# Gate weights broadcast in pieces, a projection in another order, and an attention core whose second pass begins at another tile

## The chip, the cores and the metric

One core of one Trainium2 chip runs a two-layer model (eight residual stages) on 4 x 1024 tokens of width 128, in float32 with some bf16 operands. The metric is the device time of one execution in microseconds. The three runs of the kernel before took 3448.38, 3451.47 and 3469.87 us.

## The reference, cut to what matters

Each stage reads the normalised x and adds its result to x. The change touches three of the stages: the first attention, the mixture-of-experts FFN (used twice) and the latent attention's projection.

```
x = x + L0_attn_a(layernorm(x))   # 64 batch-heads, causal, scores + a table by distance
x = x + L0_ffn(layernorm(x))      # stage f0
x = x + L0_attn_b(layernorm(x))
x = x + L0_ffn(layernorm(x))      # stage f1
x = x + L1_attn_a(layernorm(x))   # latent attention, rotary part
...
def L0_ffn(x):                    # 8 experts, top 2, and a shared expert
    logits = x @ gate_w.T
    idx = top_2(logits + lb_bias)
    w = sigmoid(logits[idx]); w = w / (sum(w) + 1e-6)
    hidden = square(relu(x @ w1[e]))            # for every expert e
    return sum_e(we[e] * (hidden @ w2[e])) + square(relu(x @ cfc)) @ cproj
def L1_attn_a(x):
    c_q, c_kv = x @ W_DQ, x @ W_DKV
    Q = concat(c_q @ W_UQ, rope(c_q @ W_QR)); K = concat(c_kv @ W_UK, rope(x @ W_KR)); V = c_kv @ W_UV
```

## The kernel before

Every stage is a block in which the five engines run lists written out by hand, tied by counting semaphores (a wait holds up everything behind it on its engine). Between blocks there is a barrier. Tokens go in 8 groups of 512; x stays in SBUF.

**First attention core** (`attention_two_pass`, L1028; tiles named l0aa). The 64 batch-heads go in 16 quads of 4. A first pass finds for each query the lowest score: per quad 18 tiles, each a set of matmuls into a bank of 128x1024 (`first_pass`, L1183) and one reduction on DVE (`first_lows`, L1346, L1350). Eight small reductions, a transpose and three parts in bf16 (`second_lows`, `parts`, `remainder`, `remainder_low` with L1377) turn the result into rows that a DMA puts under the queries. The second pass has 36 steps a quad (`second_pass`, L1221): scores into one of three banks, Exp on ACT (L1322) for three heads of four, then a multiplication by the table on POOL (L1179: one instruction for heads 0 and 1, one for head 2); for the fourth head DVE adds the table first (L1344). `weigh` multiplies by v. The lists of PE and DVE place one tile of the next quad's first pass in every second step, 20 steps ahead (AHEAD); so before step 0 all 18 tiles of quad 0 and 10 tiles of quad 1 are done.

**FFN of layer 0** (`l0_ffn`, L340; f0 and f1). Per group: normalisation (`ln_first`, `ln_second`), a transpose, logits, a gate of 18 small DVE steps (`gate_first`, `gate_second`, `gate_weights`), and `weights_T`, `to_weT`: the gate weights, transposed, go to DRAM (L388) and come back broadcast to all partitions in one DMA of 2 MB (L392, wB). For each of 9 units n: `up` on PE, `relu` and `square` on ACT, `weigh` by wB on DVE (L458), `down` on PE three units later. Groups 0 and 1 are gated before the loop; group g + 2 is gated within group g. In f0, SP first issues the loads of the next stage's weights and of the layer-1 FFN's (`ahead`: L998, L143), then serves the gate weights.

**Latent projection** (`l1a_project`, L2703; l1ap). Per group: PE makes the latents (pL), rotary parts (pR, pS), q, k, v and the transposes of the next group's x; DVE normalises the next group, combines the rotary parts (t1, t2, L2801 and L2802) and with ACT splits q, k and r into three bf16 parts, which SP sends to DRAM (L1010; in four groups it also loads heads, L2881).

Of the kernel before, what the change touches and what calls it, by code (L numbers as in the profile page):

```python
# [17 lines left out]
ACT = mybir.ActivationFunctionType  # L18
# [83 lines left out]
def ln_group_vector(nc, dve, src, out, S, steps, rough_ready, rough_want, ve_ready):  # L102

    for k in range(GROUP_BLOCKS):
        ins = nc.vector.bn_stats(S["st"][:, k, :], src(k))  # L105
    steps.done(ins)
    ln_variance(nc, S, steps, ve_ready)
    ln_newton(nc, dve, S, steps, rough_ready, rough_want)
    return ln_apply(nc, src, out, S)

# [229 lines left out]
def l0_ffn(nc, D, x, C, tag, we_dram, ahead=None):  # L340
# [6 lines left out]
    with ExitStack() as ctx:  # L347
# [27 lines left out]
        we_out, we_in = [sem("we_out0"), sem("we_out1")], [sem("we_in0"), sem("we_in1")]  # L375
# [5 lines left out]
        @block.sync  # L381
        def _(sp):
            if ahead is not None:
                ahead(sp)
            for g in range(GROUPS):
                par = g % 2
                sp.wait_ge(weT_ready, g + 1)
                sp.dma_start(we_dram[par], weT[:, par, :]).then_inc(we_out[par], 16)  # L388
                sp.wait_ge(we_out[par], 16 * (g // 2 + 1))
                if g >= 2:  # L390
                    sp.wait_ge(wb_used, (g - 1) * E)
                sp.dma_start(wB[:, par], we_dram[par:par + 1].broadcast_to([P, E, GROUP])).then_inc(we_in[par], 16)  # L392
# [8 lines left out]
        def _(dve):  # L401
# [49 lines left out]
            def weigh(g, e):  # L451
                n = g * HT + e
                dve.wait_ge(s_ready, n + 1)
                if e == 0:
                    dve.wait_ge(we_in[g % 2], 16 * (g // 2 + 1))
                if n >= RING:
                    dve.wait_ge(hT_used, n - RING + 1)
                nc.vector.tensor_tensor(hT[:, n % RING, :], rT[:, n % RING, :], wB[:, g % 2, e, :], ALU.mult).then_inc(wb_used, 1)  # L458
# [6 lines left out]
            for gn in (0, 1):  # L465
                lns, gs = Steps(dve, ln_step, LN_STEPS, gn), Steps(dve, g_step, G_STEPS, gn)
                ln_first(lns, gn)
                ln_second(lns, gn)
                gate_first(gs, gn)
                gate_second(gs)  # L470
                gate_weights(gs, gn)
# [26 lines left out]
        def _(act):  # L498
# [38 lines left out]
            to_weT(1)  # L537
            for n in range(3, N):
                relu(n)
                g, f = n // HT, n % HT  # L540
                if f == 1 and 1 <= g and g + 1 < GROUPS:
                    to_weT(g + 1)
                square(n)
                if g + 2 < GROUPS:
                    if f == 4:
                        to_xt(g + 2)
                    if f == 6:
                        gate_sigmoid(g + 2)

        @block.tensor  # L550
        def _(pe):
# [50 lines left out]
            weights_T(1)  # L602
            for n in range(3, N):
                g, f = n // HT, n % HT
                up(n)
                down(n - LAG)
                if g >= 1 and f == 1 and g + 1 < GROUPS:
                    weights_T(g + 1)
                if g + 2 < GROUPS:
                    if f == 3:  # L610
                        transposes(g + 2)
                    if f == 5:
                        logits(g + 2)
# [414 lines left out]
def attention_two_pass(nc, C, D, tag, qs, ks, qd, kd, qm, km, table, rows, v_all, cx, den, mask):  # L1028
# [38 lines left out]
    ADDED = 3  # L1067
    with ExitStack() as ctx:
# [113 lines left out]
        def _(pe):  # L1182
# [75 lines left out]
            for t in range(AHEAD // 2):  # L1258
                first_pass(1, t)
                if t == 1:  # L1260
                    turn_lows(0)
            for n in range(RING - 1):
                second_pass(n)
            for n in range(N):
                if n % 2 == 0:
                    quad, t = (n + AHEAD) // STEPS + 1, (n + AHEAD) % STEPS // 2
                    if quad < QUADS:
                        first_pass(quad, t)
                if n + RING - 1 < N:
                    second_pass(n + RING - 1)  # L1270
                if n % STEPS == STEPS - AHEAD + 3 and n // STEPS + 1 < QUADS:
                    turn_lows(n // STEPS + 1)
                if n % QUAD == 3 and n >= 2 * QUAD - 1:
                    weigh(n // QUAD - 1)
# [62 lines left out]
        def _(dve):  # L1337
# [44 lines left out]
            for t in range(AHEAD // 2):  # L1382
                first_lows(1, t)
                if t == 1:
                    remainder(0)
                    remainder_low(0)
            for n in range(N):
                after, more = n % STEPS - (STEPS - AHEAD), n // STEPS + 1 < QUADS
                if after == 0 and more:
                    second_lows(n // STEPS + 1)  # L1390
                if n % 2 == 0:
                    quad, t = (n + AHEAD) // STEPS + 1, (n + AHEAD) % STEPS // 2
                    if quad < QUADS:
                        first_lows(quad, t)
                if after == 5 and more:
                    remainder(n // STEPS + 1)
                if after == 8 and more:
                    remainder_low(n // STEPS + 1)
                if n % QUAD == ADDED:
                    add_table(n)  # L1400
# [1302 lines left out]
def l1a_project(nc, D, x, C, tag, v_all, dram, ahead):  # L2703
# [3 lines left out]
    with ExitStack() as ctx:  # L2707
# [17 lines left out]
        xt = sb("xt", [P, GROUP])  # L2725
# [57 lines left out]
        def _(dve):  # L2783
            for par in (0, 1):
                dve.sem_inc(sent[par], 16 * SENDS)
            def layernorm(gn, par):
                steps = Steps(dve, ln_step, LN_STEPS, gn)
                dve.wait_ge(xT_done, gn + 1)
                ln_group_vector(nc, dve, lambda k: x[:, bass.ds((gn + 1) * GROUP_BLOCKS + k, 1), :], xn[:, par], S, steps,
                                ln_rough, gn + 1, ln_ve).then_inc(xn_ready, 1)  # L2790
                steps.close()

            layernorm(0, 0)
            dve.wait_ge(w_in, 16 * NW)
            with dve.Fori(0, BATCH) as b:
                for par in (0, 1):
                    g = b * 2 + par
                    t = slice(par * GROUP, (par + 1) * GROUP)
                    layernorm(g + 1, 1 - par)
                    dve.wait_ge(done["r"], g + 1)  # L2800
                    nc.vector.tensor_tensor(t1[:], pR[0:R, :], cos[:, t], ALU.mult)  # L2801
                    nc.vector.tensor_tensor(t2[:], pS[0:R, :], sin[:, t], ALU.mult).then_inc(rope, 1)  # L2802
                    dve.wait_ge(rope, g + 2)
# [14 lines left out]
        def _(act):  # L2818
            def to_xt(gn):
                act.wait_ge(xT_done, gn + 3)  # L2820
                nc.scalar.activation(xt[:], pT[:], ACT.Copy).then_inc(xt_ready, 1)

            to_xt(0)
            with act.Fori(0, BATCH) as b:
                for par in (0, 1):
# [5 lines left out]
                    for n in "qk":  # L2831
                        act.wait_ge(done[n], g + 1)
                        nc.scalar.activation(part[n][:, par, 0, :], src[n][:], ACT.Copy).then_inc(hi[n], 1)
                    act.wait_ge(r_ready, g + 1)
# [4 lines left out]
                    to_xt(g + 1)  # L2839

        @block.tensor
        def _(pe):
# [11 lines left out]
            with pe.Fori(0, BATCH) as b:  # L2854
                for par in (0, 1):
                    g = b * 2 + par
                    pe.wait_ge(xt_ready, g + 1)
                    nc.tensor.matmul(pL[0:L, :], wl[:], xt[:], start=True, stop=True).then_inc(lat_done, 1)
# [9 lines left out]
                    nc.tensor.matmul(pK[:], wuk[:], lat[:], start=True, stop=True).then_inc(done["k"], 1)  # L2868
                    pe.wait_ge(v_ready, g + 1)
# [3 lines left out]
                    transposes(g + 1, 1 - par)  # L2873
# [298 lines left out]
def build(nc, D, out):  # L3172
    with ExitStack() as ctx:
# [39 lines left out]
        with ExitStack() as stages:  # L3213
# [3 lines left out]
            def ahead(sp):  # L3217
                load_l0_attn_b(sp, D, C, W)
                load_l1_ffn(sp, D, C)

            l0_ffn(nc, D, x, C, "f0", we, ahead=ahead)
            l0_attn_b(nc, D, x, C, W, "l0b")
        l0_ffn(nc, D, x, C, "f1", we)
# [113 lines left out]
```

## Time and profile before

| | us |
|---|---|
| median of 3 runs | 3451.47 (3448.38 to 3469.87) |
| profiled execution: time, span | 3457.46, 3455.7 |
| first attention core, second pass | 236 to 757 |
| f0, f1 | 900 to 1077, 1396 to 1560 |
| latent projection | 1560 to 1676 |
| mean TensorE clock of the span | 0.93 of full |

All times are from the start of the span of one profiled execution. PE is TensorE's matmuls, PEld its weight loads, DVE VectorE, ACT ScalarE, POOL GpSimd, SP SyncE. In a timeline a row stands for one instruction or for a run of like ones (x8), with the idle time of the engine just before it in brackets and what ended that. [...]

### The profile page before, as it was taken

The page shows a single profiled execution, that of the slowest core. Times are in us where ns is not written, and L with a number is a line of the kernel's source. Part 1 is how long each engine was busy: PE and PEld are TensorE (multiplying, and loading weights), DVE is VectorE, ACT ScalarE, POOL GpSimd, SP SyncE. Part 2 cuts the span into 40 slices and gives each one's busy share as a digit, 9 for nine tenths or more (in the row PEclk, how much of TensorE's full clock was granted, in tenths as well). Part 3 has the DMA queues.
Part 4 walks back from the last instruction along what each step waited for, and adds up shares of the span by engine and source line. Part 5 has one row for each costly group of instructions (what it writes and reads, how often), then busy time and mean ns, then how long its engine had stood idle before and what let it go on. Part 6 is the DMA issues. An engine that isn't in the chain of part 4 may idle for free. (4 is left out here: it accounts for less than half of the span.)

```text
span 3455.7 us, 67058 instructions
## 1 busy us (share of the span) xinstructions
PE 3053.0 (88%) x25109; PEld 1677.9 (49%) x25109; DVE 2373.2 (69%) x5084; ACT 1862.5 (54%) x3317; POOL 945.4 (27%) x655
## 2 busy tenths in 40 slices
PE   6778999958599999896799969998999999999899
PEld 3234444423276555573222237764455555555676
DVE  6578888848574554666799942235999999998321
ACT  5336666642264332463599924443666666666444
POOL 1029999971001322000000000001222223232100
PEclk8779999989798999897799969999999999999999
DMA  5212333210330000224322210017434344332000
GB/s 169 71 63 94 106 118 109 91 54 24 104 123 25 1 1 1 99 99 157 106 68 67 62 44 1 1 35 219 112 88 99 98 105 106 97 100 68 12 10 13
DMA packets 215138, 260.69 MB, mean 75 GB/s; under 512 B 45211, under 2 KB 165604, under 8 KB 212497
## 3 DMA queue, kind: packets, MB, share of 16 engines
q1 hardware_dynamic: 214849, 256.83, 25.0%
q8 instruction: 183, 3.00, 0.4%
q14 instruction: 106, 0.86, 0.1%
HBM read 200.72 MB, written 56.55 MB: 74 GB/s over the span
## 5 line engine op out<-in xcount | busy, mean ns | idle before, releaser
L1179 POOL TENSOR_TENSOR l0aa_e<-l0aa_e,l0aa_et 128x1024 f32<-128x1024 f32 (+1 forms) x288 | 512.0, 1816 | 44.6 <-ACT l0aa_e L1322 44.5
L2597 ACT ACTIVATE l1ba_sg<-l1ba_sg,l1ba_mn 128x128 f32<-128x128 f32 (+7 forms) x512 | 394.4, 774 | 185.3 <-DVE l1ba_mn L2649 184.2
L2649 DVE CUSTOM_DVE_ANT_0 l1ba_sg<-l1ba_pS,l1ba_tab 128x128 f32<-128x128 f32 (+7 forms) x512 | 368.0, 743 | 40.9 <-PE l1ba_pS L2538 28.5
L1350 DVE TENSOR_REDUCE l0aa_low<-l0aa_pP 128x8 f32<-128x1024 f32 x288 | 343.2, 1220 | 65.8 <-PE l0aa_pP L1203 61.8
L2659 DVE STREAM_TRANSPOSE l1ba_pT<-l1ba_sg 128x1024 f32<-128x1024 f32 (+3 forms) x344 | 367.1, 1067 | 18.5 <-ACT l1ba_sg L2597 13.5
L319 PEld LDWEIGHTS f_pY<-l_w,f_hT 128*128 128x128 f32 x2048 | 268.8, 192 | 122.9 <-issue 119.5
L2559 PE MATMUL l1ba_pO<-l1ba_pT,l1ba_v 32*64 32x256 f32 x9216 | 320.0, 389 | 7.8 <-ACT l1ba_y L2612 7.8
L3027 ACT ACTIVATE l1aa_e<-l1aa_e 128x1536 f32<-128x1536 f32 x192 | 284.4, 1483 | 33.3 <-DVE l1aa_e L3070 21.0
L282 ACT ACTIVATE f_hT<-f_pH,l_b 128x512 f32<-128x512 f32 x256 | 173.9, 687 | 237.4 <-PE f_pH L311 237.2
L2482 POOL TENSOR_TENSOR l1ba_co<-l1ba_co,l1ba_rb 128x1024 f32<-128x1024 f32 x64 | 151.5, 2367 | 544.3 <-ACT l1ba_co L2605 512.5
L1322 ACT ACTIVATE l0aa_e<-l0aa_pS 128x512 f32<-128x512 f32 x432 | 243.0, 593 | 87.0 <-PE l0aa_pS L1236 48.4
L319 PE MATMUL f_pY<-l_w,f_hT 128*128 128x128 f32 x2048 | 269.9, 275 | 0.7 <-ACT f_hT L282 0.7
L311 PE MATMUL f_pH<-f_xt,l_w 128*128 128x512 f32 x512 | 268.1, 608 | 0.0
L2559 PEld LDWEIGHTS l1ba_pO<-l1ba_pT,l1ba_v 32*64 32x64 f32 x9216 | 176.5, 132 | 177.4 <-issue 144.4
L3070 DVE SCALAR_TENSOR_TENSOR l1aa_e<-l1aa_pS,l1a_ceiling 128x1536 f32<-128x1536 f32 x128 | 214.8, 1749 | 5.6 <-PE l1aa_pS L2987 5.6
L1233 PE MATMUL l0aa_pS<-l0a_qs,l0a_ks 128*128 128x512 bf16 (+3 forms) x768 | 191.3, 332 | 30.6 <-DVE l0aa_e L1344 16.8
L1196 PE MATMUL l0aa_pP<-l0a_ks,l0a_qs 96*128 96x512 bf16 (+3 forms) x768 | 186.5, 347 | 28.0 <-DVE l0aa_rest L1372 13.4
L2987 PE MATMUL l1aa_pS<-l1a_qs,l1a_ks 72*128 72x512 bf16 (+3 forms) x768 | 165.5, 341 | 38.1 <-DVE l1aa_e L3068 13.6
L2538 PE MATMUL l1ba_pS<-l1b_k,l1ba_qs 64*128 64x448 f32 (+2 forms) x768 | 178.5, 545 | 17.8 <-DVE l1ba_mn L2649 17.8
L590 PEld LDWEIGHTS f_pY<-l_w,f_hT 128*128 128x128 f32 x1152 | 152.4, 194 | 79.0 <-issue 64.7
L1250 PE MATMUL l0aa_pO<-l0aa_e,l0aa_vh 128*32 128x512 f32 (+3 forms) x1536 | 155.1, 499 | 10.6 <-POOL l0aa_e L1179 10.6
L590 PE MATMUL f_pY<-l_w,f_hT 128*128 128x128 f32 x1152 | 153.1, 278 | 10.8 <-DVE f_hT L458 10.8
(407 smaller groups left out, 5103.2 us busy)
## 6 DMA issues: line engine op xcount, KB each, us to landing
f_wB<-l0f_weights SPq DMA_DIRECT2D x16, 2048.0 KB, 7.2
l1ba_rb<-l1b_rdd SPq DMA_DIRECT2D x64, 512.0 KB
l0aa_et<-l0a_table SPq DMA_DIRECT2D x16, 1536.0 KB
l1b_qd<-l1bp_part SPq DMA_DIRECT2D x64, 256.0 KB, 2.4
l1ba_qs<-l1b_qd SPq DMA_DIRECT2D x48, 256.0 KB
l0aa_et<-l0a_table SPq DMA_DIRECT2D x16, 512.0 KB
l1ba_tab<-l1b_table SPq DMA_DIRECT2D x32, 256.0 KB
l1ba_qs<-l1b_qd SPq DMA_DIRECT2D x64, 128.0 KB
```

The lines of the kernel that those rows point to most:

```text
L311: nc.tensor.matmul(pH[n % RING][:], w1[:, n % HT, :], xt[:, n // HT % 2, :], start=True, stop=True).then_inc(h_done, 1)
L319: ins = nc.tensor.matmul(pY[g % 2][:, k * P:(k + 1) * P], hT[:, n % RING, k * P:(k + 1) * P], w2[:, f, :], start=(f == 0 and k == 0), stop ...
L590: ins = nc.tensor.matmul(pY[g % 2][:, k * P:(k + 1) * P], hT[:, n % RING, k * P:(k + 1) * P], w2[:, f, :], start=(f == 0 and k == 0), stop ...
L1179: nc.gpsimd.tensor_tensor(es, es, t, ALU.mult).then_inc(multiplied, heads)
L1322: nc.scalar.activation(e[:, n % E_SLOTS, :], pS[n % RING][:], ACT.Exp, scale=-1.0).then_inc(e_done, 1)
L1350: nc.vector.tensor_reduce(low1[:, t, :], pP[TURN[quad, t]][:].rearrange("p (u t) -> p u t", t=P), AX.X, ALU.min).then_inc(p1_low, 1)
L2559: ins = nc.tensor.matmul(pO[a][part * HALF:(part + 1) * HALF, 0:HG * Q], v4[a * Q:(a + 1) * Q, group_of(r)[0] % 2, (SEQ - width(r)) // Q + ...
L2597: nc.scalar.activation(row, row, ACT.Exp, bias=mn[:, r % 2, i + k:i + k + 1], scale=-1.0, accum_out=den[:, r % 2, i + k:i + k + 1]).then_i ...
L2649: nc.vector.tensor_tensor_reduce(row, scores, bias, 1.0, 3e38, ALU.add, ALU.min, mn[:, r % 2, h:h + 1]).then_inc(m_done, 1)
L2659: nc.vector.transpose(pT[tile][:, c + i * width(r):c + (i + heads) * width(r)], sg[:, n % RING, 0:heads * width(r)]).then_inc(t_done, 1)
L3027: nc.scalar.activation(es, es, ACT.Exp, scale=1 / ROOT).then_inc(e_done, 1)
L3070: ins = nc.vector.scalar_tensor_tensor(es, pS[s % 2][:], -CLIP, ceiling[:, unit - 1, :], ALU.max, ALU.min)
```

## The change

Three edits. In the attention core, 6 tiles of quad 1's first pass (before: 10) precede step 0, and steps 0 to 7 hold one tile each; from step 8 on the order is as before. In `l0_ffn`, wB comes in four DMAs of two experts with a semaphore each; DVE computes group 1's statistics before group 0's gate; `weights_T(1)` moves from before unit 3 to unit 4, and in group 0 the transposes and logits of group 2 move two units later; the `ahead` loads are issued after the last gate weights, those of the layer-1 FFN now in f1. In `l1a_project`, DVE's normalisation is cut in two around t1 and t2, the transposes precede v, xt has two buffers, and the copy to it comes before the r part on ACT.

```diff
@@ l0_ffn
-        we_out, we_in = [sem("we_out0"), sem("we_out1")], [sem("we_in0"), sem("we_in1")]
+        we_out = [sem("we_out0"), sem("we_out1")]
+        we_in = [[sem(f"we_in{par}_experts{e}") for e in range(0, E, 2)] for par in (0, 1)]
...
-            if ahead is not None:
-                ahead(sp)
             for g in range(GROUPS):
...
-                sp.dma_start(wB[:, par], we_dram[par:par + 1].broadcast_to([P, E, GROUP])).then_inc(we_in[par], 16)
+                for e in range(0, E, 2):
+                    sp.dma_start(wB[:, par, e:e + 2], we_dram[par:par + 1, e:e + 2].broadcast_to([P, 2, GROUP])).then_inc(we_in[par][e // 2], 16)
+            ahead(sp)
...
-                if e == 0:
-                    dve.wait_ge(we_in[g % 2], 16 * (g // 2 + 1))
+                if e % 2 == 0:
+                    dve.wait_ge(we_in[g % 2][e // 2], 16 * (g // 2 + 1))
...
-            for gn in (0, 1):
-                lns, gs = Steps(dve, ln_step, LN_STEPS, gn), Steps(dve, g_step, G_STEPS, gn)
-                ln_first(lns, gn)
-                ln_second(lns, gn)
-                gate_first(gs, gn)
-                gate_second(gs)
-                gate_weights(gs, gn)
+            lns, gs = ([Steps(dve, step, n, gn) for gn in (0, 1)] for step, n in ((ln_step, LN_STEPS), (g_step, G_STEPS)))
+            ln_first(lns[0], 0)
+            ln_second(lns[0], 0)
+            ln_first(lns[1], 1)
+            gate_first(gs[0], 0)
+            gate_second(gs[0])
+            gate_weights(gs[0], 0)
+            ln_second(lns[1], 1)
+            gate_first(gs[1], 1)
+            gate_second(gs[1])
+            gate_weights(gs[1], 1)
@@ l0_ffn, scalar
             gate_sigmoid(1)
-            to_weT(1)
             for n in range(3, N):
                 relu(n)
                 g, f = n // HT, n % HT
-                if f == 1 and 1 <= g and g + 1 < GROUPS:
+                if f == (1 if g else 4) and g + 1 < GROUPS:
                     to_weT(g + 1)
                 square(n)
                 if g + 2 < GROUPS:
-                    if f == 4:
+                    if f == (4 if g else 6):
                         to_xt(g + 2)
-                    if f == 6:
+                    if f == (6 if g else 7):
                         gate_sigmoid(g + 2)
@@ l0_ffn, tensor
             logits(1)
-            weights_T(1)
             for n in range(3, N):
                 g, f = n // HT, n % HT
                 up(n)
+                if n == 4:
+                    weights_T(1)
                 down(n - LAG)
...
-                    if f == 3:
+                    if f == (3 if g else 5):
                         transposes(g + 2)
-                    if f == 5:
+                    if f == (5 if g else 7):
                         logits(g + 2)
@@ attention_two_pass
+    EARLY = 6
+    def tile_at(n):
+        if n < AHEAD - 2 * EARLY:
+            return 1, EARLY + n
+        if n % 2 == 0 and (n + AHEAD) // STEPS + 1 < QUADS:
+            return (n + AHEAD) // STEPS + 1, (n + AHEAD) % STEPS // 2
+        return None
... (tensor; vector has the same with first_lows)
-            for t in range(AHEAD // 2):
+            for t in range(EARLY):
                 first_pass(1, t)
...
-                if n % 2 == 0:
-                    quad, t = (n + AHEAD) // STEPS + 1, (n + AHEAD) % STEPS // 2
-                    if quad < QUADS:
-                        first_pass(quad, t)
+                if tile_at(n):
+                    first_pass(*tile_at(n))
@@ l1a_project
-        xt = sb("xt", [P, GROUP])
+        xt = sb("xt", [P, 2, GROUP])
... (vector)
-                    layernorm(g + 1, 1 - par)
+                    steps = Steps(dve, ln_step, LN_STEPS, g + 1)
+                    ln_statistics(nc, rows(g + 1), S, steps, ln_ve)
                     dve.wait_ge(done["r"], g + 1)
                     nc.vector.tensor_tensor(t1[:], pR[0:R, :], cos[:, t], ALU.mult)
                     nc.vector.tensor_tensor(t2[:], pS[0:R, :], sin[:, t], ALU.mult).then_inc(rope, 1)
+                    normalise(g + 1, 1 - par, steps)
                     dve.wait_ge(rope, g + 2)
... (scalar: after the two "hi" copies of q and k)
+                    to_xt(g + 1, 1 - par)
                     act.wait_ge(r_ready, g + 1)
...
                         nc.scalar.activation(part[n][:, par, 1, :], f[n][:], ACT.Copy).then_inc(mid[n], 1)
-                    to_xt(g + 1)
... (tensor)
                     nc.tensor.matmul(pK[:], wuk[:], lat[:], start=True, stop=True).then_inc(done["k"], 1)
+                    transposes(g + 1, 1 - par)
                     pe.wait_ge(v_ready, g + 1)
...
-                    transposes(g + 1, 1 - par)
@@ build
-            def ahead(sp):
-                load_l0_attn_b(sp, D, C, W)
-                load_l1_ffn(sp, D, C)
-
-            l0_ffn(nc, D, x, C, "f0", we, ahead=ahead)
+            l0_ffn(nc, D, x, C, "f0", we, lambda sp: load_l0_attn_b(sp, D, C, W))
             l0_attn_b(nc, D, x, C, W, "l0b")
-        l0_ffn(nc, D, x, C, "f1", we)
+        l0_ffn(nc, D, x, C, "f1", we, lambda sp: load_l1_ffn(sp, D, C))
```

## Rows read from the trace of the kernel before

**Rows 1.** Window over the second pass: length, busy PE, PEld, DVE, ACT, POOL, then PEclk.
```profile
236.00:757.00 521.00, 465.81 (x3744) 210.00 (x3741) 430.99 (x554) 344.58 (x648) 512.00 (x288) 0.98 0.28 91
```

**Rows 2.** Timeline of POOL, first attention core: start, us, instruction [idle before <-releaser].
```profile
236.34 27.17 POOL L1179 TENSOR_TENSOR l0aa_e<-l0aa_e,l0aa_et 128x1024 f32<-128x1024 f32 x15 [35.98 <-ACT l0aa_e L1322]
266.99 1.26 POOL L1179 TENSOR_TENSOR l0aa_e<-l0aa_e,l0aa_et 128x512 f32<-128x512 f32 x1 [3.47 <-ACT l0aa_e L1322]
269.82 3.60 POOL L1179 TENSOR_TENSOR l0aa_e<-l0aa_e,l0aa_et 128x1024 f32<-128x1024 f32 x2 [1.58 <-ACT l0aa_e L1322]
...
295.17 421.85 POOL L1179 TENSOR_TENSOR l0aa_e<-l0aa_e,l0aa_et 128x1024 f32<-128x1024 f32 x237 [0.26 <-ACT l0aa_e L1322]
```

**Rows 3.** Timeline of DVE, four stretches of the same stage.
```profile
225.93 9.95 DVE L1350 TENSOR_REDUCE l0aa_low<-l0aa_pP 128x8 f32<-128x1024 f32 x8 [0.51 <-PE l0aa_pP L1203]
...
257.95 5.71 DVE L1377 TENSOR_TENSOR l0aa_mp<-l0aa_rest,l0aa_mp 32x128 bf16<-32x128 f32 x1
...
296.95 0.72 DVE L1377 TENSOR_TENSOR l0aa_mp<-l0aa_rest,l0aa_mp 32x128 bf16<-32x128 f32 x1
...
707.54 9.62 DVE L1377 TENSOR_TENSOR l0aa_mp<-l0aa_rest,l0aa_mp 32x128 bf16<-32x128 f32 x1
```

**Rows 4.** Timelines of PE and ACT, the same stage.
```profile
234.41 1.06 PE L1233 MATMUL l0aa_pS<-l0a_qs,l0a_ks 128*128 128x512 bf16 x2
235.26 0.78 PE L1196 MATMUL l0aa_pP<-l0a_ks,l0a_qs 96*128 96x512 bf16 x3
...
254.94 1.08 ACT L1322 ACTIVATE l0aa_e<-l0aa_pS 128x512 f32<-128x512 f32 x2 [0.75 <-PE l0aa_pS L1236]
```

**Rows 5.** Timeline of all engines, start of f0 (SPq: SP's DMA issues).
```profile
911.67 9.61 SPq L143 DMA_DIRECT2D l_w<-in_L_ffn_w  x2
...
914.39 0.87 DVE L407 BATCH_NORM_STATS2 f_ln_stats<-x 128x6 f32<-128x128 f32 x4
...
915.39 0.57 ACT L511 ACTIVATE f_weT<-f_pT 8x512 f32<-8x512 f32 x1
...
926.69 0.19 DVE L448 TENSOR_TENSOR f_we<-f_sg,f_mx 128x32 f32<-128x32 f32 x1
...
929.62 0.33 SPq L388 DMA_DIRECT2D l0f_weights<-f_weT  x1
...
932.55 0.33 SPq L392 DMA_DIRECT2D f_wB<-l0f_weights  x1
...
939.76 0.69 DVE L458 TENSOR_TENSOR f_hT<-f_rT,f_wB 128x512 f32<-128x512 f32 x1 [11.35 <-DMA f_wB<-l0f_weights]
```

**Rows 6.** The same, second FFN.
```profile
1420.79 0.19 DVE L448 TENSOR_TENSOR f_we<-f_sg,f_mx 128x32 f32<-128x32 f32 x1
...
1422.41 0.69 DVE L458 TENSOR_TENSOR f_hT<-f_rT,f_wB 128x512 f32<-128x512 f32 x1
...
1430.27 0.97 PEld L565 LDWEIGHTS f_pG<-l_gw,f_xt 128*128 128x128 f32 x8
...
1432.95 0.69 DVE L458 TENSOR_TENSOR f_hT<-f_rT,f_wB 128x512 f32<-128x512 f32 x1
...
1434.90 0.69 DVE L458 TENSOR_TENSOR f_hT<-f_rT,f_wB 128x512 f32<-128x512 f32 x1
```

**Rows 7.** Timelines of DVE, PE and SP, latent projection: groups 2 and 3 of 0 to 7.
```profile
1598.01 0.16 DVE L89 TENSOR_TENSOR l1ap_ln_newton<-l1ap_ln_rstd 128x4 f32<-128x4 f32 x1 [1.12 <-POOL l1ap_ln_rstd L2776]
...
1599.84 0.68 DVE L2801 TENSOR_TENSOR l1ap_t<-l1ap_pR,l1ap_cos 68x512 f32<-68x512 f32 x1
...
1605.42 2.02 PE L2858 MATMUL l1ap_pL<-l1ap_xt,l1ap_wl 128*100 128x512 f32 x2 [3.71 <-ACT l1ap_xt L2821]
...
1606.49 2.24 SPq L1010 DMA_DIRECT2D l1a_kc<-l1ap_partk  x3
```

**Rows 8.** Windows over those two groups, columns as in the windows above.
```profile
1594.90:1605.40 10.50, 6.04 (x22) 2.92 (x22) 9.13 (x29) 4.73 (x8) 1.01 (x1) 0.95 0.61 190
1605.40:1618.80 13.40, 10.18 (x23) 4.13 (x23) 9.52 (x30) 4.46 (x8) 1.01 (x1) 0.66 0.83 281
```

More of the change, by code:

```diff
@@ L109, in ln_group_vector, with ln_statistics @@
     return ln_apply(nc, src, out, S)
+def ln_statistics(nc, src, S, steps, ve_ready):
+    for k in range(GROUP_BLOCKS):
+        ins = nc.vector.bn_stats(S["st"][:, k, :], src(k))
+    steps.done(ins)
+    ln_variance(nc, S, steps, ve_ready)
 LN_STEPS = 6
@@ L337, in _, with l0_ffn @@
                 down(n)
-def l0_ffn(nc, D, x, C, tag, we_dram, ahead=None):
+def l0_ffn(nc, D, x, C, tag, we_dram, ahead):
     E = 8
@@ L1381, in _ @@
             second_lows(0)
-            for t in range(AHEAD // 2):
+            for t in range(EARLY):
                 first_lows(1, t)
@@ L1390, in _ @@
                     second_lows(n // STEPS + 1)
[L1391 to L1394, printed above, removed]
+                if tile_at(n):
+                    first_lows(*tile_at(n))
                 if after == 5 and more:
@@ L2785, in _, with rows, normalise @@
                 dve.sem_inc(sent[par], 16 * SENDS)
-            def layernorm(gn, par):
-                steps = Steps(dve, ln_step, LN_STEPS, gn)
+            def rows(gn):
+                return lambda k: x[:, bass.ds((gn + 1) * GROUP_BLOCKS + k, 1), :]
+            def normalise(gn, par, steps):
+                ln_newton(nc, dve, S, steps, ln_rough, gn + 1)
                 dve.wait_ge(xT_done, gn + 1)
-                ln_group_vector(nc, dve, lambda k: x[:, bass.ds((gn + 1) * GROUP_BLOCKS + k, 1), :], xn[:, par], S, steps,
-                                ln_rough, gn + 1, ln_ve).then_inc(xn_ready, 1)
+                ln_apply(nc, rows(gn), xn[:, par], S).then_inc(xn_ready, 1)
                 steps.close()
-            layernorm(0, 0)
+            steps = Steps(dve, ln_step, LN_STEPS, 0)
+            ln_statistics(nc, rows(0), S, steps, ln_ve)
+            normalise(0, 0, steps)
             dve.wait_ge(w_in, 16 * NW)
@@ L2818, in _, with to_xt @@
         def _(act):
-            def to_xt(gn):
+            def to_xt(gn, par):
                 act.wait_ge(xT_done, gn + 3)
-                nc.scalar.activation(xt[:], pT[:], ACT.Copy).then_inc(xt_ready, 1)
-            to_xt(0)
+                nc.scalar.activation(xt[:, par, :], pT[:], ACT.Copy).then_inc(xt_ready, 1)
+            to_xt(0, 0)
             with act.Fori(0, BATCH) as b:
@@ L2857, in _ @@
                     pe.wait_ge(xt_ready, g + 1)
-                    nc.tensor.matmul(pL[0:L, :], wl[:], xt[:], start=True, stop=True).then_inc(lat_done, 1)
+                    nc.tensor.matmul(pL[0:L, :], wl[:], xt[:, par, :], start=True, stop=True).then_inc(lat_done, 1)
                     pe.wait_ge(rope, g + 1)
```

## The prediction, made before the change was run

> **What bounds the kernel now.** No engine bounds the whole span, so I read the three touched stages one by one: first the windows for the busiest engine, then that engine's timeline for what ended its idle time, then the engine that released it.
>
> In the attention core the window [rows 1] has PE at 466 of 521 us, but POOL at 512.0, and the timeline of POOL [rows 2] shows it without a pause for 421.85 us. PE's 466 is pipelined matmuls, so POOL is the bound: the stage lasts as long as POOL's start (236.34), its 512.0 of work, and its few pauses. They all follow one instruction. L1377, a 32x128 operation on DVE, takes 0.72 us at 296.95 but 5.71 at 257.95 and 9.62 at 707.54 [rows 3]; both long ones end just as POOL's run ends (27.17 us after 236.34), and POOL then sits idle 3.47 + 1.58 us for want of Exp output [rows 2]. DVE was held until POOL had run dry.
>
> In f0 the timeline of all engines [rows 5] is read backwards: the first `weigh` (939.76) waited 11.35 us for wB; wB was issued at 932.55, after gate weights sent at 929.62, which ACT had ready at 915.39 + 0.57. In between SP stood in the loads of other stages. In f1, with no loads, the same `weigh` follows the gate by 1.4 us [rows 6]: there DVE's chain bounds the start.
>
> In the latent projection DVE is busy 9.1 of 10.5 us of a group at full clock; at 0.66 of it the group takes 13.4 [rows 8]. DVE's idle time has the wait for POOL's power (1.12 us) and PE has 3.71 us before pL, waiting for the copy of xt that ACT makes last [rows 7].
>
> **Attention core.** Eight reductions take 9.95 us, 1.24 each [rows 3], and tiles 6 to 9 no longer stand before step 0: POOL starts 5.0 us earlier, at 231.4. But DVE keeps all its work: steps 0 to 7 hold eight reductions and two additions, 1.4 us a step, while POOL needs 0.9 (1.78 an instruction, two in four steps [rows 2]). So POOL starves and DVE's progress sets what follows. DVE itself slips: PE still runs at half clock (two second-pass matmuls in 1.06 us [rows 4]), and tile 6 waits behind three of them. In the row at 235.26 the clock is already up, one microsecond after the second pass began; if it rises as soon, DVE slips 0.3, if it stays down for four steps 2.8. I take 1.5. POOL's instruction for steps 24 and 25 then starts when their Exp ends, 254.94 + 1.08 + 1.5 = 257.6, hardly before the 257.64 of now (236.34 + 12 x 1.78). Up to there the edit gives nothing.
>
> The gain would come from L1377. Now it begins 0.3 us after the start of a POOL instruction and waits 5.7. In quad 2 it begins 296.95 - 295.17 = 1.8 after one, at a point where POOL had just waited for ACT [rows 2], and waits until that instruction's end, 0.7. A starved POOL starts right after Exp, 257.95 - 256.02 = 1.9 before L1377: the case of quad 2. I take the short wait and save 5.05 us of idle POOL; with the pauses left, the stage ends 5.2 us earlier (bounds: 6.6 saved, 0.5 lost if the wait stays).
> [...]
>
> **FFN, f0.** SP is free when ACT has the weights (915.96). Out and back took 932.55 - 929.62 = 2.9, landing 939.76 - 932.55 = 7.2 for 2 MB whole: at latest 926.1, a quarter sooner. DVE: moving group 1's statistics to the idle time before the logits saves their 2.6 us (914.39 to the end of POOL's power at 917.0); gate 1 ends at 926.88 - 2.6, and `weigh` follows 1.4 later as in f1: 925.7. The first `weigh` comes 14.0 us earlier. Against it: in group 0 the logits come two units later. From them to the end of `weigh` 5 is 1432.95 + 0.69 - 1430.27 = 3.4 us [rows 6], of which PE covers 1.4 with the logits and one `up`; it idles 2.0, and I add 0.4 for the next two units, where gate steps and `weigh` take 1434.90 - 1432.95 = 1.95, a little more than PE's unit. `weights_T(1)`, until now in idle time, lies behind the first `down`: four transposes, by the logits' eight loads (0.97 at full clock) 0.5, doubled at half clock, 0.9. f0: 14.0 - 3.3 = **10.7 earlier** (bounds 9 and 12.5: the gate chain fully exposed, or hidden).
> **f1** gains only 2.0 at the start (the transposes wait for weT) and 0.6 of a pause of PE, and pays 3.3: **0.7 later** (bounds 1 earlier, 1.5 later).
> SP: three more issues of 0.33 us a group lie beside 17 us of PE ((1077 - 940) / 8). The moved loads start after the last wB, early in group 6, and so about 30 us before a stage ends. Those of f0 took SP from 900 to 911.67, those of the layer-1 FFN to 929.62: 12 and 18 us, hidden by group 7. If that cover failed, PE would wait for the rest.
>
> **Latent projection.** At full clock the wait for POOL (1.12) goes behind t1 and t2; for the r part, which comes later on ACT, I add 0.3: 10.5 becomes 9.7. At half clock pL starts early, but pR and pS take twice its 2.02 us, less the overlap 3.4, and end 1.6 after DVE's statistics, and v's doubled time delays its copy by 1.3: 9.7 + 2.9 = 12.6 for 13.4. In the first group nothing started early, and the normalisation no longer fills DVE's wait for pS: 1599.84 - 1598.01, about 2.0. Now the two kinds alternate, 12.0 a group on the mean. PE's long pause of 3.7 us, after which the low group came, is cut into two of 1.7, so I expect the clock up more often, 10.4 a group: 7 x 1.6 - 2.0 = **9 earlier** (bounds: always up 14, always down 6 later). SP's sends (four runs up to 2.24 us [rows 7], in four groups also loads) fill about 10 us, which keeps it from less.
>
> **Sum.** 5.2 + 10.7 - 0.7 + 9 = 24.2. The profiled execution took 3457.46 us, 6.0 above the median of 3451.47: 3427 as a median.
>
> **Rivals.**
> The wait at L1377 stays in quad 1 (for it: two of the three starts outside the regular phase were long): 5.7 more, 3433, chance 0.2.
> The clock in the projection goes on alternating or stays low (PE is busy for some 60% of a group either way): it gives 4, or loses 6: 3432 to 3442; chance 0.2.
> The loads are late for the next stage (for it: the loads of both together occupied SP for 29 us): f0's gain would shrink by up to 14: 3441, chance 0.05.
> Slower: the changed start leaves the steady state in another phase, in which L1377 waits 5 us in each quad; 5.5 x 14 = 77: 3504. It decides from 11 such quads. Against it, after the upset at 257.95 quad 2 was already regular. Chance 0.05.
> All bounds on the good side, 34 less: 3417; chance 0.1. The rest, 0.4, is the forecast.
>
> **Numbers.** The range takes in the first three rivals but the worst of the second and the good bounds, and 3 to 6 us for the spread of the runs (3448 to 3470): 3411 to 3447. About 1%, 34.5 us, is what a measurement can tell from no change. Faster by more than that needs nearly every bound at its good end: 0.12. Slower: 0.05. Within: 0.83.
>
> **What would show it.** POOL's first multiplication at 231 to 232 and L1377 of quad 1 under 1 us; if it is long, POOL's pauses stay. In f0 the first `weigh` about 11 us after ACT's weT, ended by DVE's own chain and not by a DMA; a pause of PE near 2 us before `down` 5 in both FFNs. In the projection no idle time before L89, and groups of 9.7 to 10.5 us with PEclk near 1. The forecast is wrong if wB still ends the wait in f0, if later quads have long L1377s, or if the next stage's first matmul waits for a load.

## The result, and the profile after

| | kernel before | kernel after | |
|---|---|---|---|
| median, us | 3456.04 (9 runs, 3441.42 to 3469.92) | 3434.14 (9 runs, 3420.19 to 3441.67) | ratio 0.9927, 95% 0.9904 to 0.9950 |
| profiled execution, us | 3457.46 | 3436.40 | 21.1 less |
| its attention core, us | 571.60 | 565.13 | -6.5 (forecast -5.2) |
| its f0, us | 177.95 | 165.60 | -12.4 (forecast -10.7) |
| its f1, us | 165.09 | 164.98 | -0.1 (forecast +0.7) |
| its latent projection, us | 114.68 | 105.31 | -9.4 (forecast -9) |
| all other stages, us | 2426.4 | 2433.6 | +7.2 (untouched) |

The ratio stands for 25 us (17 to 33), while the two medians lie 21.9 apart; the forecast of 24.2 is 0.9930, and the ratio's value stays within the 1% to which I gave 0.83. A stage is counted from its first instruction to the next stage's first. The touched stages gave 28.3 us, and 7.1 of that went in the table stage ahead of the core, in which nothing was changed: its loop took 7.3 us a turn at half clock (0.50 granted) and 3.8 at full (1.00), and the clock rose 14.6 us later in the stage than in the profile of before (97.5 us before, 104.5 after; in twelve more profiles 96.8 to 104.6). So below I compare stage lengths, not totals, except where runs were repeated. A second set of runs of the same kernel gave 3431.40 us, ratio 0.9935 (0.9910 to 0.9961).

**Attention core.** Timeline of POOL over its first quad, then DVE at the subtraction of quad 1 and of the last quad (L1398 now, L1377 before), as in [rows 2] and [rows 3]; this core began at 205.33, the one before at 197.38:
```profile
239.26 3.56 POOL L1202 TENSOR_TENSOR l0aa_e<-l0aa_e,l0aa_et 128x1024 f32<-128x1024 f32 x2 [30.95 <-ACT l0aa_e L1343]
243.93 3.63 POOL L1202 TENSOR_TENSOR l0aa_e<-l0aa_e,l0aa_et 128x1024 f32<-128x1024 f32 x2 [1.10 <-ACT l0aa_e L1343]
249.05 3.65 POOL L1202 TENSOR_TENSOR l0aa_e<-l0aa_e,l0aa_et 128x1024 f32<-128x1024 f32 x2 [1.49 <-ACT l0aa_e L1343]
252.89 10.68 POOL L1202 TENSOR_TENSOR l0aa_e<-l0aa_e,l0aa_et 128x1024 f32<-128x1024 f32 x6 [0.19 <-ACT l0aa_e L1343]
264.19 37.93 POOL L1202 TENSOR_TENSOR l0aa_e<-l0aa_e,l0aa_et 128x1024 f32<-128x1024 f32 x21 [0.62 <-ACT l0aa_e L1343]
...
720.26 1.26 POOL L1202 TENSOR_TENSOR l0aa_e<-l0aa_e,l0aa_et 128x512 f32<-128x512 f32 x1 [2.34 <-ACT l0aa_e L1343]
...
265.97 0.72 DVE L1398 TENSOR_TENSOR l0aa_mp<-l0aa_rest,l0aa_mp 32x128 bf16<-32x128 f32 x1
...
708.45 9.62 DVE L1398 TENSOR_TENSOR l0aa_mp<-l0aa_rest,l0aa_mp 32x128 bf16<-32x128 f32 x1
```
POOL begins 33.9 us after the core does, where it was 39.0, waits for Exp in the first quad (3.4 us in four pauses, where it had run 27 us without one), and the subtraction of quad 1 takes 0.72 us instead of 5.71. The one of the last quad is as long as ever, and POOL idles 2.34 us behind it.

**FFN f0.** The timeline of all engines at the places of [rows 5]; f0 began at 901.80 (900.13 before):
```profile
917.06 0.57 ACT L524 ACTIVATE f_weT<-f_pT 8x512 f32<-8x512 f32 x1
917.66 0.28 SPq L395 DMA_DIRECT2D l0f_weights<-f_weT  x1
...
919.13 1.75 SPq L400 DMA_DIRECT2D f_wB<-l0f_weights  x4
919.37 1.14 PEld L577 LDWEIGHTS f_pG<-l_gw,f_xt 128*128 128x128 f32 x8 [0.92 <-ACT f_xt L514]
...
924.65 0.19 DVE L457 TENSOR_TENSOR f_we<-f_sg,f_mx 128x32 f32<-128x32 f32 x1
...
926.28 0.69 DVE L467 TENSOR_TENSOR f_hT<-f_rT,f_wB 128x512 f32<-128x512 f32 x1
...
940.07 0.69 DVE L467 TENSOR_TENSOR f_hT<-f_rT,f_wB 128x512 f32<-128x512 f32 x1
...
940.81 2.08 PE L602 MATMUL f_pY<-l_w,f_hT 128*128 128x128 f32 x8 [1.40 <-DVE f_hT L467]
```
SP sends the weights as soon as ACT has them, the first `weigh` (926.28) follows DVE's own chain and no DMA ends its wait. Then `down` 5 (940.81) waits 1.40 us for `weigh` 5 behind group 2's gate, and it runs at half clock (2.08 us for what takes 1.05 at full). In f1 `down` 5 waits 1.39 us and takes 1.71.

**Latent projection.** Windows over two groups, one at full clock and one with the clock partly down, columns as in [rows 8] (the third figure from the end is PEclk, the clock granted to TensorE as a share of full); then PE's and DVE's waits in it:
```profile
1593.74:1603.11 9.37, 6.06 (x23) 2.86 (x22) 9.13 (x29) 4.45 (x8) 1.01 (x1) 0.98 0.90 271
1603.11:1614.16 11.05, 7.76 (x23) 3.25 (x22) 9.15 (x29) 4.45 (x8) 1.01 (x1) 0.86 0.86 296
```
```profile
1596.45 0.15 DVE L89 TENSOR_TENSOR l1ap_ln_newton<-l1ap_ln_rstd 128x4 f32<-128x4 f32 x1
...
1598.40 0.66 PE L2871 MATMUL l1ap_pT<-ident,l1ap_xn 128*128 128x128 f32 x4 [1.48 <-DVE l1ap_xn L97]
...
1602.68 1.87 PE L2888 MATMUL l1ap_pR<-l1ap_lat,l1ap_wr 100*68 100x512 f32 x2 [1.83 <-ACT l1ap_lat L2853]
```
DVE is busy 9.13 of 9.37 us, no wait for POOL is left at L89, and PE's pause of 3.71 us is now two of 1.48 and 1.83. The clock is down 3.4 us in each 20.5, where it was down 10.2 in each 23.9; over the whole stage it was down 33.9 of 105.3 us, before 57.4 of 114.7.

### The profile page after: what moved, and what is told of

It is laid out like the page before. It is cut to its first block and busy times, and to the rows that moved or that the text cites. A ratio compares the mean times of both kernels' runs of the same rounds, so it can differ in the third digit from the quotient of the medians.

```text
span 3434.6 us, 67066 instructions
## 1 busy us (share of the span) xinstructions
PE 3040.1 (89%) x25048; PEld 1669.9 (49%) x25109; DVE 2365.7 (69%) x5084; ACT 1861.6 (54%) x3317; POOL 945.6 (28%) x655
## 5 line engine op out<-in xcount | busy, mean ns | idle before, releaser
L1256 PE MATMUL l0aa_pS<-l0a_qs,l0a_ks 128*128 128x512 bf16 (+3 forms) x707 | 175.3, 324 | 29.0 <-ACT l0aa_e L1343 13.5
L1273 PE MATMUL l0aa_pO<-l0aa_e,l0aa_vh 128*32 128x512 f32 (+3 forms) x1536 | 155.0, 499 | 10.9 <-POOL l0aa_e L1202 10.8
```

## Experiments

All but the pair under **Both mended** were executed once, so their stage lengths carry what follows and their totals only stand here. Beside one execution of the kernel before at 3473.38 us: the core's edit 3458.15, the loads moved 3437.40, the pieces 3458.92, DVE's order in the projection 3478.01. Beside one at 3450.19: the projection's whole edit 3453.97, group 0's order as before 3423.08, the subtraction shifted 3436.20, the remainder in PSUM 3429.55. Beside eleven with a median of 3453.63: the projection's early half 3447.17, four tiles 3438.82. How little one total says is plain from the projection's whole edit: its stage was 9.7 us shorter than in the profile of before and its total 3.8 longer than the execution beside it.

**The core's edit alone.** Kernel before with `EARLY = 6` and `tile_at`, nothing else.

> The kernel before with the edit of the attention core alone (six tiles before step 0, the other four one a step). My theory, that the edit works only through the two-SBUF subtraction of quad 1 (L1377 in the kernel before), expects the core's length as in the kernel after, 565 us from its first to the next stage's first instruction instead of 572, POOL's first multiplication about 34 us after the core begins (39 before), and 0.7 us instead of 5.7 for that subtraction; the other stages keep their lengths (f0 178, f1 165, latent projection 115). The rival, that POOL's earlier start itself gives the time, expects a length of 567 even if the subtraction still takes 5.7 us. Total 5 to 7 us below the kernel before, within what one run shows.

The core took 564.8 us, POOL began 33.9 us after it, the subtraction took 0.72 us; f0 178.0, f1 165.1, projection 114.7. As forecast. The rival was not ruled out by this run but by the next one.

**Only SP's loads moved.**
```diff
             for g in range(GROUPS):
 ...
                 sp.dma_start(wB[:, par], ...)
+            ahead(sp)
```


> The kernel before with the loads of the next stages behind SP's loop in both FFNs, and nothing else: wB in one piece of 2 MB, DVE's and PE's order as before. My theory: SP alone was late; wB then lands 2.9 + 7.2 us after ACT has group 0's weights, and the first weigh starts about 28 us after f0 begins, ended by DVE's gate chain, 11.4 us earlier than in the kernel before; with the unit order as before there is no new pause before down 5, so f0 takes 166 to 167 us of 178, about as much as the whole change gave (165.6). The rival, that four pieces are needed, expects the first weigh to wait for wB and f0 at 169 or more. f1 stays at 165.

Timeline of this kernel's f0, begun at 894.18, then of POOL and DVE in its core, which has no edit:
```profile
909.44 0.57 ACT L511 ACTIVATE f_weT<-f_pT 8x512 f32<-8x512 f32 x1
...
911.52 0.33 SPq L391 DMA_DIRECT2D f_wB<-l0f_weights  x1
...
920.73 0.19 DVE L448 TENSOR_TENSOR f_we<-f_sg,f_mx 128x32 f32<-128x32 f32 x1
920.96 0.88 DVE L407 BATCH_NORM_STATS2 f_ln_stats<-x 128x6 f32<-128x128 f32 x4
...
922.37 0.69 DVE L458 TENSOR_TENSOR f_hT<-f_rT,f_wB 128x512 f32<-128x512 f32 x1
...
234.04 66.32 POOL L1179 TENSOR_TENSOR l0aa_e<-l0aa_e,l0aa_et 128x1024 f32<-128x1024 f32 x37 [35.98 <-ACT l0aa_e L1322]
...
256.74 1.07 DVE L1377 TENSOR_TENSOR l0aa_mp<-l0aa_rest,l0aa_mp 32x128 bf16<-32x128 f32 x1
```
The first `weigh` comes 28.2 us into f0 behind DVE's chain, and f0 takes 165.9 us: moving the loads gives 12.0 of the 12.4 us that the whole edit gave. What else was edited in f0 nets next to nothing: with all of it f0 took 164.4 to 165.6 us in four profiles.

The core brought a test that I had not planned. With ten tiles in front as before, its subtraction of quad 1 took 1.07 us this time, POOL ran through the first quad without a pause, and the core took 566.2 us, 5.4 less than in the profile of before. The edited core takes 564.8 to 565.1. A second old core with a short wait took 566.4. So the 5.0 us of POOL's earlier start leave 1.1 to 1.6 of their own, and 5.2 to 5.4 are the short wait, which the old core has only sometimes (1.07 and 1.08 us in two of its six profiles; 4.62, 5.58, 5.71 and 5.78 in four), while the edited one had it in each of eight (0.72; seven with six tiles, one with four). The six old cores took 569.5 us on the mean, so on the mean the edit gives 4.5.

**Only the pieces of wB,** with the loads still in front.

> The kernel before with wB in four pieces of 512 KB, each with its own semaphore, and the loads still in front of the loop. My theory: SP still stands in the loads until 29.5 us after f0 begins, so the first weigh comes only 2 us earlier (a piece lands in 5.2 us where the whole took 7.2): f0 at 176 of 178 us. The rival, that the pieces give the gain, expects 170 or less. f1 unchanged (165), where wB has landed before the first weigh.

f0 took 175.0 us: 3.0 less, not 2. The first `weigh`, at 37.1 us into f0, still waited 8.85 us for the DMA. The pieces are 512 KB in 5.1 us (median) where the whole was 2 MB in 7.2, but the first `weigh` needs only the first piece, and that landed 4.0 us after its issue: my 2 us had been worked out from the median. Once SP is free the pieces have nothing left to give at the start of f0: an estimate for a whole wB in the kernel after, from its issue at 919.13 - 901.80 = 17.3 and the landing time before, is 17.3 + 7.2 = 24.5 us into f0, and DVE's chain ends there at 24.5. The rival fell.

**The projection's halves.** First DVE's order alone.
```diff
-                    layernorm(g + 1, 1 - par)
+                    ln_statistics(nc, rows(g + 1), S, steps, ln_ve)
 ... (t1, t2)
+                    normalise(g + 1, 1 - par, steps)
```


> The kernel before with only DVE's order changed in the latent projection: statistics, then the two products of the r part, then the rest of the normalisation; transposes and the copy of xt stay at the end of the group, with one xt. My theory (most of the gain comes from PE's start: its pause of 3.7 us before the latent matmul is what lets the clock fall) expects groups of about 10 us at full clock but the clock still down in every second group, the stage at 110 us or more (115 before, 105 after). The rival, that the wait for POOL was what mattered (1.1 us in each of 8 groups), expects 106.

Windows over two groups of this kernel, and PE's waits in the first:
```profile
1592.60:1606.39 13.79, 10.28 (x23) 4.09 (x22) 9.09 (x29) 4.60 (x9) 1.01 (x1) 0.62 0.47 145
1606.39:1620.18 13.79, 10.21 (x23) 4.12 (x22) 9.10 (x29) 4.66 (x9) 1.01 (x1) 0.62 0.53 155
...
1598.03 2.03 PE L2871 MATMUL l1ap_pL<-l1ap_xt,l1ap_wl 128*100 128x512 f32 x2 [2.73 <-ACT l1ap_xt L2834]
```
The stage took 127.9 us, 13 more than before: the clock was down in every group (PEclk 0.62; 81.1 of the stage's 127.9 us), and six of eight took 13.79 us. "110 or more" held, but I had not foreseen a loss. Then the whole edit, alone:

> The kernel before with the whole edit of the latent projection and nothing else. The stage should take 105 us as in the kernel after (115 before), with groups of 9.4 us at full clock and 11.0 where the clock is down for 3.4 us; the difference to the DVE order alone is what the early transposes and the double xt give. Rival: the stage's clock in the kernel after came from what ran ahead of it; then 109 or more. All other stages as in the kernel before (core 572, f0 178, f1 165).

105.0 us, groups of 9.38 at full clock and 10.4 to 10.9 else: what runs ahead of the stage is not the reason. Then the other half, transposes and the copy of xt early, DVE's order as before:

> The kernel before with only the other half of the projection's edit: transposes and the copy of xt before v's matmuls, with two xt, while DVE normalises in one go ahead of the r part. With the DVE order alone the stage took 127.9 us (115 before, 105 with both), with the clock down in all groups. My theory: PE's starting early is what keeps the clock up, and the DVE order is worth only the 1.1 us wait for POOL in each group: 105 + 8 x 1.1 less what the first group loses, so 110 to 113 us, with full-clock groups of 10.5 and the clock down for 3.4 us at a time. The rival, that the two halves only work together, expects 115 or more.

Window over one group of it:
```profile
1600.00:1610.55 10.55, 6.07 (x22) 2.83 (x22) 9.18 (x29) 4.73 (x8) 1.01 (x1) 1.00 0.76 227
```
106.6 us. Six of its eight groups took 10.55 us, also those in which the clock was down for 3.4: DVE's wait for POOL, 1.12 us in each group, apparently leaves the slack that hides that. At full clock a group takes as long as it did in the kernel before (10.55), so the early half alone gives its 8.1 us in the groups in which the clock is down: they took 13.3 us before. Over the stage the clock was down 46.0 of 106.6 us. The stage with both halves took 102.7 to 106.8 us in eight profiles (median 104.2), so a gain of DVE's order on top is not shown: it costs 13 us alone, and the 2 us between 106.6 and the median are less than the stage's own spread. My "110 to 113" was too high, since I had counted the low groups as longer.

**PE's and ACT's order in group 0 as before,** the rest as in the kernel after.
```diff
-                if f == (1 if g else 4) and g + 1 < GROUPS:
+                if f == 1 and 1 <= g and g + 1 < GROUPS:
 ...
             logits(1)
+            weights_T(1)
 ...
-                if n == 4:
-                    weights_T(1)
 ...
-                    if f == (5 if g else 7):
+                    if f == 5:
                         logits(g + 2)
```


> The kernel after with PE's and ACT's order in group 0 of the FFN as it was before (weights_T(1) and its copy ahead of the loop, transposes, logits and sigmoid of group 2 at units 3 to 6); DVE's order, the pieces and the moved loads stay. My theory: the later logits cost a pause of PE of 1.4 + about 1.5 us in slower clock in each FFN, and weights_T(1) fits in PE's idle time before the first down: f0 162 to 163.5 us of 165.6, f1 162 to 163.5 of 165.0, total 4 to 6 us below the kernel after. The rival: PE is then held by weights_T(1) before up 3, and both stages stay as in the kernel after (within 0.5 us).

Timeline of this kernel, f0 begun at 896.17:
```profile
919.22 0.19 DVE L457 TENSOR_TENSOR f_we<-f_sg,f_mx 128x32 f32<-128x32 f32 x1
...
919.47 1.01 PE L586 MATMUL f_pT<-ident,f_we 128*8 128x128 f32 x4 [4.28 <-DVE f_we L457]
...
920.28 1.91 PE L592 MATMUL f_pH<-f_xt,l_w 128*128 128x512 f32 x2
...
920.85 0.69 DVE L467 TENSOR_TENSOR f_hT<-f_rT,f_wB 128x512 f32<-128x512 f32 x1
...
931.00 0.69 DVE L467 TENSOR_TENSOR f_hT<-f_rT,f_wB 128x512 f32<-128x512 f32 x1
```
f0 took 162.5 us and f1 161.0: 3.1 and 4.0 less than in the profile of after. Over all profiles f0 takes 164.4 to 165.6 with the late units and 162.5 to 162.7 without, f1 164.1 to 165.0 and 161.0 to 162.0, so the gain is 1.7 to 3.2 and 2.1 to 4.0 us. `weights_T(1)` fits into PE's wait of 4.28 us, `weigh` 5 (931.00) comes 34.8 us into f0 where it came after 38.3, and PE no longer stands before `down` 5. So in the FFN the moved units were the part of the change that only cost.

**Where the subtraction is issued.** It sits at another step in eight quads of the kernel after.
```diff
-                if after == 8 and more:
+                if more and after == LOW_AT[n // STEPS + 1]:
                     remainder_low(n // STEPS + 1)
```


> The kernel after with the two-SBUF subtraction (L1398 in the kernel after) issued at another step in each second quad: at 7, 9, 10, 11, 12, 9, 10, 11 after the second lows for quads 2, 4, 6, 8, 10, 12, 14, 15; the odd quads but the last at 8 as now, as controls. [...] Theory B (only an arrival within a few tenths of a microsecond of a POOL instruction's start is passed over): short, up to 2.4 us, at most positions, long at one or two. Theory C (the second to issue waits for one instruction only): at most 2.4 us everywhere, the core unchanged.

Timeline of DVE: the two long ones, in quad 3 (a control, at 8) and the last (at 11); then POOL around the first:
```profile
321.13 4.42 DVE L1399 TENSOR_TENSOR l0aa_mp<-l0aa_rest,l0aa_mp 32x128 bf16<-32x128 f32 x1
...
708.62 2.58 DVE L1399 TENSOR_TENSOR l0aa_mp<-l0aa_rest,l0aa_mp 32x128 bf16<-32x128 f32 x1
...
311.21 14.20 POOL L1203 TENSOR_TENSOR l0aa_e<-l0aa_e,l0aa_et 128x512 f32<-128x512 f32 x8
328.87 1.26 POOL L1203 TENSOR_TENSOR l0aa_e<-l0aa_e,l0aa_et 128x512 f32<-128x512 f32 x1 [3.47 <-ACT l0aa_e L1344]
```
Steps 9 and 11 hold no work of their own on DVE, so they turned out to be the places of 8 and 10 over again (0.73 and 0.78 us at 9, 0.86 at 11 in quad 8); 7 gave 0.56 us, 10 gave 0.83 twice, 12 gave 0.95. All of these end 0.14 to 0.15 us after the end of the POOL instruction under way. That DVE gets in only at the end of a POOL instruction which had itself waited for its data does not hold: at 10 and 12 the instruction under way had had its data 0.5 to 0.8 us before it began. Theory C falls: 4.42 us runs past two ends of POOL instructions. Theory B doesn't hold as I wrote it: the long wait in quad 3 began 1.6 us after the start of one. Although it is a control, it came there earlier than its like: in the steady course of all 14 profiles the subtraction arrives 1.70 to 1.78 us into a POOL instruction, 184 times, and none of these took over 0.80 us. And the last quad, with the same order on DVE and the same arrival 0.08 us before POOL's next start, took 2.58 us here and 9.62 in the kernel after. The core took 570.6 us, 5.5 more than in the kernel after: the long wait in quad 3 emptied POOL for 3.47 + 1.58 us, the pattern of [rows 2], and 1.2 in small pauses behind it; position 12 made a row late, which PE awaited for 1.89 us and POOL for 1.68; and the pause of 2.84 us in the last quad was gone.

**The last remainder in PSUM.**
```diff
+        def rest_of(quad):
+            return pP[TURN[quad, NT]][0:QUAD * U, P:2 * P] if quad == QUADS - 1 else rest[:]
 ... (remainder, middle_parts and remainder_low use rest_of(quad) for rest[:])
```


> The kernel after with the last quad's remainder kept in PSUM instead of SBUF (its bank has no other user then), so that the last subtraction has one SBUF input and one in PSUM. [...]

DVE and POOL at the last quad:
```profile
699.83 0.27 DVE L1401 TENSOR_TENSOR l0aa_mp<-l0aa_pP,l0aa_mp 32x128 bf16<-32x128 f32 x1
...
680.92 65.06 POOL L1205 TENSOR_TENSOR l0aa_e<-l0aa_e,l0aa_et 128x512 f32<-128x512 f32 x37
```
0.27 us for 9.62, no pause of POOL, and the core took 561.5 us, 3.6 less, where I had expected POOL's idle 2.34 + 0.5 = 2.84. The other two profiles with the remainder in PSUM, below, have 0.27 as well, while with both inputs in SBUF the last subtraction took 0.27 in one profile of eleven, 2.58 in one and 9.62 to 9.67 in nine. For this instruction the only difference between the two groups is one input in PSUM, so the long time goes with the second input in SBUF. Of the 3.6 us some 0.8 are more than POOL's pause and stay unexplained.

**Both mended.** The two edits above together; with the kernel after beside it on the same chip.

> The kernel after once more, beside the combined kernel on one chip, as the base for it. Expected: ratio to the kernel before 0.993 (0.990 to 0.996), about 24 us.

> The kernel after with the unit order of group 0 as before the change in both FFNs (as in units_back) and the last remainder in PSUM (as in low_in_psum). The parts measured alone as stage lengths: 3.6 us in the attention core (565.1 to 561.5), 3.1 in f0 (165.6 to 162.5), 4.0 in f1 (165.0 to 161.0). They lie in different stages, so they should add: 10.7 us below the kernel after, ratio to the kernel before 0.990 (0.987 to 0.993), about 3422 us where the kernel before takes 3456. The rival, that run-to-run changes of the clock in untouched stages eat it, expects the ratio not below 0.992.

After: 3431.40 us, ratio 0.9935 (0.9910 to 0.9961). Combined: 3421.31 us (6 runs, 3419.30 to 3432.29), ratio 0.9908 (0.9882 to 0.9934), against 3453.63 for the kernel before. The difference of the medians is 10.1 us for 10.7 expected; the intervals of the two ratios overlap, and the stage lengths carry the claim: core 561.5, f0 162.5, f1 162.0. Against the profile of the kernel after beside it (564.8, 164.4, 164.1) that is 7.4 us and not 10.7, since I had taken each part from a single pair of profiles. The ratio's rival ("not below 0.992") fell by its point value only, since the interval reaches to 0.9934. This version has the lowest median of all.

**Four tiles instead of six,** in the combined kernel (`EARLY = 4`).

> The combined kernel with four tiles instead of six before step 0 of the attention core. My theory, that DVE's work sets the first quad's course and that POOL's earlier start is given back as idle time: POOL begins about 31.5 us after the core's first instruction (34 with six tiles, 39 with ten), its idle time in the first quad grows from 3.0 to about 5.5, the core stays at 561.5 within 0.7, provided that the subtraction of quad 1 stays short. The rival, that the earlier start is the gain, expects 559.

PE and SP at the second pass's start; this core began at 204.85:
```profile
234.00 0.42 PE L1229 MATMUL l0aa_pP<-l0a_mask,ident 128*128 128x128 bf16 x2
236.75 1.04 PE L1259 MATMUL l0aa_pS<-l0a_qs,l0a_ks 128*128 128x512 bf16 x2 [2.33 <-DMA l0a_qs<-l0a_rows]
...
234.42 0.25 SPq L1148 DMA_DIRECT2D l0a_qs<-l0a_rows  x1
```
POOL began 33.8 us after the core did, not 31.5, its idle time grew from 3.1 to 5.3, and the core took 563.8 us, 2.3 more. I had left out a term: the second pass needs the row of quad 0, which lands 2.3 us after the fourth tile is through. Six tiles just fill that wait; with four the remaining tiles come later for nothing.

## Why the prediction was right

The time (3427 forecast, 3434.1 and 3431.4 measured; 24.2 us against 25 by the ratio and 21.9 by the medians) came out of the stages that I had named, in nearly the sizes. That the totals agree so closely is partly luck: in the profiles the four stages gave 28.3 us, 4 more than the sum, and untouched stages took 7.2 back.

**Core.** POOL's start 5.0 us earlier: measured 5.0. "Up to there the edit gives nothing; the gain comes from L1377, 5.05": measured 5.2 to 5.4 for the short wait, from profiles of the same old core with and without it, and 1.1 to 1.6 for the rest, which I had put at 0.15. Missing in my working was that the old core's wait is not fixed: in two of six profiles it was short. So the edit gains 1.3 us against some executions of the old core and 6.7 against others. The first rival (the wait stays) didn't occur in eight profiles of the edited core: the subtraction came 1.78 us into POOL's instruction in each, as quad 2's did before, for 1.9 forecast. The control in quad 3 shows that the same issue step is hit when it arrives at 1.62. Why 1.70 to 1.78 is safe was a guess from one row, and remains without a cause.

**f0.** The wait for wB went as worked out, though the first `weigh` came 9.2 us after ACT's weT began and not the 11 that I had named as a sign. Two terms were mis-sized or misjudged. DVE's earlier statistics gave more than 2.6: the first `weigh` came 3.5 us earlier (28.19 with the loads alone, 24.68 with units back) and 3.8 in f1, among other things because group 1's logits now fall in the stretch at full clock (1.14 us of loads, 1.78 before). The late units cost 3.1 and 4.0 in these profiles (1.7 to 4.0 over all) against my 3.3. Both errors have the same sign in f0, hence 12.4 instead of 10.7, and cancel in f1. The pause before `down` 5 was 1.40 us where I had put 2.0, so in these profiles more of the late units' price than I had given it lies in the slower clock and in `weights_T(1)`; which of the two, no run shows. The larger point is one of attribution: nothing but the loads was needed for f0's 12 us.

**Projection.** 9.4 us for 9 (7.9 to 12.0 over the profiles with the edit), by compensation. Forecast: 9.7 at full clock and 12.6 at half, 10.4 on the mean. Measured: 9.37 and 11.0, 10.2 on the mean, since between the first group and the last the clock fell for only 3.4 us in every second group; the first group cost 14.2 us where it had 12.5, a loss of 1.7 for the 2.0 forecast. That PE's long pause was what let the clock down is not shown. For it: with both halves PE's longest pause in the steady groups is 1.83 us, and the clock is down for less of the stage. Against it: with DVE's order alone PE paused 2.66 to 3.48 us before pL, less than the 3.71 of the kernel before, and the clock was down for more (81.1 us against 57.4); with the early half alone pauses of up to 3.1 us were left, and it was down for less (46.0). The halves change PE's load as well as its pauses, so what the clock goes by is left open.

**Loads moved behind.** They begin right after the last wB, as worked out, and the issues end well ahead of the stage's end (timeline of SP; then the next stage's first matmul on PE):
```profile
1039.01 0.62 SPq L1011 DMA_DIRECT2D l0b_wf<-in_L_attn_b_W_f  x1
...
1051.53 2.66 SPq L1011 DMA_DIRECT2D l0b_sel<-in_L_attn_b_sel  x1
...
1067.43 11.29 PE L950 MATMUL l0b_pA<-l0b_wf,l0b_wqkT 64*128 64x64 f32 x64 [1.63 <-PEq L60]
```
The matmul follows PE's own sequencer, as in the kernel before (1.60 us there), and no load. In f1 the loads' issues likewise begin 0.04 us after the last wB's and end at 1531.31, 17 us before the stage does. The third rival fell.

**The slower rival.** Long subtractions in every quad: in eight profiles of the edited core there was one before the last quad, in quad 3 of the kernel with shifted positions. It emptied POOL for 6.3 us with the small pauses behind it, where I had put 5.5 a quad.

## What to carry to other kernels

Before splitting a transfer, see how long its issue stood in the queue: here reordering SP's queue gave 12 us, the four pieces at most 3, and only as long as the queue was late. When a chain is moved later to make room, check whether an engine that waits anyway has the room already: PE's wait of 4.28 us took the work that had been moved away from it at a price of 2 to 4 us a stage. And judge a small edit by the lengths of its stages in several profiles: untouched stages moved by 7 us, and an unchanged instruction by 5.

## What the hardware showed that I had not expected

The subtraction, a DVE instruction with both inputs in SBUF, ended 0.14 to 0.15 us after the end of one of POOL's multiplications when it came beside them, but not always the next. The waits of 4.4 to 5.8 us passed two ends and those of 9.6 us five, and all of them ended only when POOL had no data left; the one of 2.58 us passed one. The time of arrival does not decide it to within some 10 ns: with ten tiles in front it arrived 1417 ns into a POOL instruction and took 1.07 us in one kernel, 1425 ns into the same one and took 4.62 in a second, 1431 ns and took 1.08 in a third. In the last quad it took 9.62 to 9.67 us in nine of ten profiles and 0.27 in the tenth, each time arriving about 0.1 us before POOL's next start. The runs show the wait only with POOL at work and both inputs in SBUF: in quad 0, 6 to 11 us before POOL's first multiplication, the subtraction took 0.28 us in all 14 profiles, and with one input in PSUM, beside POOL, 0.27 in three. The waits of 0.7 us lasted until the POOL instruction under way had ended, the long ones past it. What picks the end at which DVE gets in was not found: neither the readiness of POOL's data nor the place in its instruction explains it, though arrivals 1.70 to 1.78 us into one, the 184 of the steady course, were all short.
